# Attention scores from two float32r parts in two row groups, in place of three bf16 parts in one

## The chip, the cores and the metric

The kernel runs on one core of a Trainium2 chip. The metric is device time in microseconds of one launch, the median of several runs; lower is better. TensorE (PE) multiplies matrices, VectorE (DVE), ScalarE (ACT) and GpSimd (POOL) work on elements, and SyncE (SP) issues most DMAs.

## The reference

x has 4 batches of 1024 tokens of width 128. The layer is a macaron: half a mixture of experts, attention, half a mixture of experts again.

```python
x = x + 0.5 * ffn(layernorm(x), ...)      # 8 experts, top 1
q, k, v = (heads(layernorm(x) @ W.T) for W in (Wq, Wk, Wv))   # 16 heads of 8
q, k = rope(q), rope(k)
score = einsum('bqd,bkd->bqk', q, k), causal
out = softmax(score / sqrt(8)) @ v;   x = x + out @ Wo.T
x = x + 0.5 * ffn(layernorm(x), ...)
```

Everything is float32, and q and k have magnitudes at which a single bf16 product is too coarse for the scores. So the kernel splits q and k into parts whose products are exact, and adds the products in the contraction.

## The kernel before

**Three blocks run one after another**: the first expert layer (`ffn`, r=0), projection and attention (`project`, `attention`), and the second expert layer. The change touches the middle one alone, but for some memsets at the very start.

**Projection** (`project`) goes through 8 chunks of 512 tokens. PE turns a chunk (L947), multiplies it with four weight matrices for q and k (L957, float32) and one for v (L962). DVE multiplies with cosine and sine (`rotate`, L908 and L909), POOL adds the two (L1038), ACT copies the sum to bf16, which is the high part (L1008), DVE subtracts it from the sum (L917), ACT copies the rest to bf16, the middle part (L1014), and DVE (for q, L923) or POOL (for k, L1050) subtracts again for the low part. SP stores three parts of q and three of k to HBM in a layout by head (L1081).

**Attention** works in 16 stages of four heads (`QH`), each over all 1024 tokens. For a stage SP loads "stacks": `qs` and `ks` hold, for each head side by side in the free dimension, 72 rows (`PR`), in which the three parts of 8 rows are repeated so that each part of q meets each part of k. Three more rows (`MR`) of `qs` hold the negated row maximum in three bf16 parts, against ones in `ks`. Stacks have a ring of three.

Each stage does two things that are interleaved in one fixed order (`plan`):

- *tiles* for the next stage: PE computes scores with the queries on the partitions into one of two PSUM buffers `psS` (L1308), DVE adds the mask and takes the maximum of each row (L1448). There are 24 tiles: 8 of two heads with 128 to 512 keys each, 16 of one head with 640 to 1024 keys, the latter as two matmuls.
- *scores* for this stage: 12 units of 4 heads. PE computes scores transposed, maximum subtracted in the same contraction, into one of three buffers `psST` (L1339); ACT takes the exponential (L1412); POOL masks the diagonal (L1533); PE multiplies with v in float32, four heads in four groups of 32 columns (*weigh*, L1353), two units behind. ACT copies the sum out (L1418), PE turns it (L1323), DVE normalises (L1465, L1467).

POOL splits the row maxima (L1511 to L1516), PE turns them (L1316, *turn_max*), DVE copies them out (L1456), and SP moves them into the stacks' rows (`load_max`, L1272), twice a stage, once for each half of the queries. A score waits until the exponential three scores earlier is done (the buffers are three), a tile until the tile two earlier is read:

```python
                wait(pe, exp_done, s * SC + m - 2)
```
```python
        def use(index):
            wait(pe, use_read, index - 1)
```

The first score of each half waits for the maxima (`max_loaded`). Before the first stage an opening computes the tiles of stage 0; ahead of it stands a warm-up loop of fixed count on PE. ACT's first exponential waits until all parts are split (`lo_done`), because `prob` serves the projection as scratch.

Of the kernel before, what the change touches and what calls it, by code (L numbers as in the profile page):

```python
# [7 lines left out]
F32 = mybir.dt.float32  # L8
BF16 = mybir.dt.bfloat16
U32 = mybir.dt.uint32  # L10
# [22 lines left out]
KINDS = 3  # L33
PR = KINDS * KINDS * DK
MR = KINDS
CH = 512
# [121 lines left out]
def build(nc, x, Wp, Wr, br, ln, Wb1, W2, b2, const, tables, out):  # L158
    ctx = ExitStack()
    with ctx:  # L160
# [26 lines left out]

        n.ks = [sb(f"ks{i}", [PR + MR, QH * S], BF16) for i in range(RING)]
        n.qs = [sb("qs0", [PR + MR, QH * S], BF16)]
# [5 lines left out]

        n.q_dram = nc.dram_tensor("q_split", (KINDS * DK, NCH, B * H, CH), BF16, kind="Internal").ap()
        n.k_dram = nc.dram_tensor("k_split", (KINDS * DK, B * H, S), BF16, kind="Internal").ap()
# [41 lines left out]

def first_block_pool(nc, pool, n):  # L240
# [564 lines left out]
STACK_DMAS = 2 * KINDS - 1 + KINDS * NCH  # L805
# [3 lines left out]
def stack_parts(n, s, q, k):  # L809


    for c in range(KINDS):
        for first, last, at in ((c, KINDS, 0), (0, c, KINDS - c)):
            if first < last:
                here = c * PART_ROWS + at * DK
                yield (k[here:here + (last - first) * DK, :],
                       n.k_dram[first * DK:last * DK, ds(s * QH, QH), :].rearrange("d h t -> d (h t)"))
        for ch in range(NCH):
            yield (q[c * PART_ROWS:(c + 1) * PART_ROWS, ch * QH * CH:(ch + 1) * QH * CH],
                   n.q_dram[:, ch, ds(s * QH, QH), :].rearrange("d h t -> d (h t)"))  # L820
# [28 lines left out]
def project(nc, n, ctx, block):  # L849
# [7 lines left out]
    def sem(name):  # L857
# [7 lines left out]
    rot, tmp, rest = ([[n.prob[:, m, 2 * i + k, :] for k in range(2)] for i in range(2)] for m in range(3))  # L865
    part = [[sb(f"part{i}{k}", [P, KINDS, CH], BF16) for k in range(2)] for i in range(2)]
# [6 lines left out]
    proj_done, summed, hi_done, rest_done, mid_done = (  # L873
        [sem(f"{k}{i}") for i in range(2)] for k in ("proj_done", "summed", "hi_done", "rest_done", "mid_done"))
# [8 lines left out]
    def _(dve):  # L883
# [19 lines left out]
        def rotate(g, k):  # L903

            for i in range(2):
                dve.wait_ge(proj_done[i], g + 1)
                wait(dve, rest_done[i], g - 1)
# [71 lines left out]
    def _(act):  # L979
# [42 lines left out]
        for g in range(NC8):  # L1022
# [3 lines left out]
            if g >= 1:  # L1026
                mid(g - 1, (g - 1) % 2)
# [3 lines left out]
        mid(NC8 - 1, 1)  # L1031

    @block.gpsimd
    def _(pool):
# [5 lines left out]
        def subtract_hi(g, k):  # L1040
            for i in range(2):
                pool.wait_ge(hi_done[i], g + 1)
                pool.wait_ge(lo_done[i], g - 1)
                nc.gpsimd.tensor_tensor(rest[i][k], rot[i][k], part[i][k][:, 0, :],
                                        ALU.subtract).then_inc(rest_done[i], 1)

        def subtract_mid(g, k, i):

            pool.wait_ge(mid_done[i], g + 1)
            nc.gpsimd.tensor_tensor(part[i][k][:, 2, :], rest[i][k], part[i][k][:, 1, :],  # L1050
                                    ALU.subtract).then_inc(lo_done[i], 1)
# [3 lines left out]
        for g in range(NC8):  # L1055
            add_pairs(g, g % 2)
            if g >= 1:
                subtract_mid(g - 1, (g - 1) % 2, 1)
        subtract_mid(NC8 - 2, 0, 0)
        subtract_hi(NC8 - 1, 1)  # L1060
        for i in range(2):
            subtract_mid(NC8 - 1, 1, i)

    @block.sync
    def _(sp):
# [5 lines left out]
        def keep(g, k):  # L1071
            heads = slice((g - k) * (H // 2), (g - k) * (H // 2) + H)
            for i in range(2):
                sp.wait_ge(lo_done[i], g + 1)
                for m in range(KINDS):
                    rows = slice(m * DK, (m + 1) * DK)
                    if i == 0:
                        there = n.q_dram[rows, k, heads, :]
                    else:
                        there = n.k_dram[rows, heads, k * CH:(k + 1) * CH]  # L1080
                    sp.dma_start(there.rearrange("d h t -> h d t"), part[i][k][:, m, :]).then_inc(split_stored[i][k], 16)  # L1081
# [510 lines left out]
```

## Time and profile before

| | |
|---|---|
| median of 3 runs | 916.42 us (909.37 to 917.06) |
| profiled execution, first to last instruction | 855.6 us |
| outside of the span, median less span | 60.8 us |
| PE, DVE, ACT, POOL busy | 91%, 71%, 59%, 37% |
| mean granted TensorE clock | 0.945 |

The page gives one execution. The only time of that execution on record is its span; what lies around it is taken as the difference to the median. "L" numbers are lines of the kernel before. PEld is the loading of weights, which overlaps PE. A matmul's row lasts from its start to its modelled end, so that matmuls that follow each other overlap in the rows, and "x8" with one time is the union of eight. A busy PE is not necessarily a PE at its peak.

### The profile page before, as it was taken

What the parts mean: (1) busy time and instruction counts of PE and PEld (TensorE: products, weight loads), DVE (VectorE), ACT (ScalarE), POOL (GpSimd) and SP (SyncE); (2) the same over time, 40 slices, a digit from 0 to 9 for tenths busy, and PEclk for the clock granted to TensorE, in tenths of its full rate; (3) what the DMA queues carried; (4) which work ended last, traced back from release to release, by engine and by line L of the source; (5) the groups of instructions that cost most, each with busy time, mean ns of one, the idle gap of its engine ahead of it and who ended that gap; (6) DMA issues with size and microseconds to landing.
All of it is one profiled execution on the core that took longest, in us unless ns stands there. A gap on an engine that the chain in (4) does not pass through costs nothing. (4 is left out here: it accounts for less than half of the span.)

```text
span 855.6 us, 17846 instructions
## 1 busy us (share of the span) xinstructions
PE 779.7 (91%) x5570; PEld 427.9 (50%) x5570; DVE 610.9 (71%) x1919; ACT 507.4 (59%) x1229; POOL 315.4 (37%) x603
## 2 busy tenths in 40 slices
PE   9889999887899999999999999999999997689995
PEld 8888896543233333333333333333333335579884
DVE  4657774698668777788878878788787722856663
ACT  2166651673247767667667766766777684146662
POOL 6177742475104223223322422331242231056753
PEclk8699999998569999999999999999999998789998
DMA  8721113065332033033113303312320001122110
GB/s 271 270 57 50 54 33 117 23 169 159 57 57 45 14 57 57 10 49 58 34 26 57 53 6 57 58 22 36 57 41 18 3 1 34 73 70 50 52 42 26
DMA packets 27989, 51.84 MB, mean 61 GB/s; under 512 B 7552, under 2 KB 19200, under 8 KB 26496
## 3 DMA queue, kind: packets, MB, share of 16 engines
q1 hardware_dynamic: 21296, 41.04, 20.7%
q0 software_dynamic: 4096, 8.69, 3.8%
q10 hardware_dynamic: 2512, 1.06, 0.5%
q8 instruction: 43, 0.70, 0.4%
q14 instruction: 42, 0.34, 0.1%
HBM read 35.40 MB, written 14.97 MB: 59 GB/s over the span
## 5 line engine op out<-in xcount | busy, mean ns | idle before, releaser
L1448 DVE CUSTOM_DVE_ANT_0 cst<-psS,mask_row 128x768 bf16<-128x768 f32 (+7 forms) x512 | 364.7, 756 | 100.2 <-PE psS L1308 97.6
L1412 ACT ACTIVATE prob<-psST 128x512 f32<-128x512 f32 (+3 forms) x750 | 317.3, 495 | 158.9 <-PE psST L1339 155.2
L1353 PE MATMUL a_psO<-prob,vs 128*32 128x512 f32 (+3 forms) x1536 | 166.7, 506 | 2.8 <-ACT prob L1412 1.7
L1532 POOL TENSOR_TENSOR a_gate<-a_zeros 1x1 f32<-1x1 f32 x128 | 23.7, 185 | 333.7 <-ACT prob L1412 333.7
L1339 PE MATMUL psST<-a_qs,ks 75*128 75x512 bf16 (+1 forms) x480 | 123.7, 327 | 5.9 <-ACT prob L1412 3.5
L1308 PE MATMUL psS<-ks,a_qs 72*128 72x512 bf16 (+2 forms) x480 | 119.0, 337 | 5.6 <-DVE a_rowmax L1448 5.5
L777 POOL DMA_INDIRECT tok<-rows,f_there_number x64 | 61.8, 966 | 86.0 <-DVE f_number L489 42.0
L1308 PEld LDWEIGHTS psS<-ks,a_qs 72*128 72x128 bf16 x480 | 35.6, 99 | 101.1 <-DVE a_rowmax L1448 33.0
L1308 PE MATMUL psS<-ks,qs 72*128 72x512 bf16 (+3 forms) x288 | 75.8, 354 | 6.7 <-DVE a_rowmax L1448 6.5
L1533 POOL TENSOR_SCALAR_AFFINE_SELECT prob<-prob 128x512 f32<-128x512 f32 x128 | 80.3, 627 | 0.0
L1339 PE MATMUL psST<-qs,ks 75*128 75x512 bf16 (+3 forms) x270 | 73.4, 346 | 2.7 <-ACT prob L1412 1.7
L1339 PEld LDWEIGHTS psST<-a_qs,ks 75*128 75x128 bf16 x480 | 43.8, 97 | 61.4 <-ACT prob L1412 28.8
L726 ACT ACTIVATE f_xnT<-f_ps_half,gb 128x128 f32<-128x128 f32 x64 | 29.3, 458 | 54.4 <-PE f_ps_half L654 54.4
L522 DVE TENSOR_SCALAR f_hidT<-f_ps_wide,f_w1s 128x128 f32<-128x128 f32 x156 | 47.2, 345 | 18.0 <-PE f_ps_logit L663 13.7
L663 PE MATMUL f_ps_wide<-f_xnT,f_w1s 128*128 x312 | 49.7, 282 | 10.0 <-ACT f_hidT L734 5.4
L743 ACT ACTIVATE f_w1s<-w 128x516 f32 x78 | 49.7, 637 | 9.8 <-DVE f_item_ring L479 9.3
L1353 PEld LDWEIGHTS a_psO<-prob,vs 128*32 128x32 f32 x1536 | 30.6, 108 | 48.1 <-ACT prob L1412 31.6
L1308 PEld LDWEIGHTS psS<-ks,qs 72*128 72x128 bf16 x288 | 21.6, 100 | 64.5 <-DVE a_rowmax L1448 28.4
L663 PEld LDWEIGHTS f_ps_wide<-f_xnT,f_w1s 128*128 128x128 f32 x312 | 40.9, 191 | 14.1 <-issue 14.0
L673 PE MATMUL f_ps_rank<-w,f_hidT 128*128 x320 | 45.4, 285 | 0.3 <-DVE f_hidT L522 0.3
L1339 PEld LDWEIGHTS psST<-qs,ks 75*128 75x128 bf16 x270 | 25.6, 102 | 38.8 <-ACT prob L1412 17.9
L1448 DVE DVE_READ_ACCUMULATOR2_ANT a_rowmax<- 128x1 f32 x512 | 42.6, 83 | 0.0
(183 smaller groups left out, 1066.1 us busy)
## 6 DMA issues: line engine op xcount, KB each, us to landing
a_qs<-q_split SPq DMA_DIRECT2D x60, 96.0 KB
rows<-tok SPq DMA_DIRECT2D x8, 536.0 KB, 4.9
ks<-k_split SPq DMA_DIRECT2D x32, 128.0 KB
qs<-q_split SPq DMA_DIRECT2D x36, 96.0 KB
q_split<-p_part SPq DMA_DIRECT2D x24, 128.0 KB, 2.4
k_split<-p_part SPq DMA_DIRECT2D x24, 128.0 KB, 2.4
ks<-k_split SPq DMA_DIRECT2D x16, 192.0 KB
tok<-x_after_first SPq DMA_DIRECT2D x4, 536.0 KB, 5.4
```

The costliest lines, as they stand in the source:

```text
L522: last = nc.vector.tensor_scalar(hidT[i % 2][:, f * P:(f + 1) * P], hidden_at(i, f), w1s[i % 4][:, F + f:F + f + 1], 0.0, ALU.add, ALU.max)
L663: last = nc.tensor.matmul(hidden_at(i, f), w1s[i % 4][:, f * P:(f + 1) * P], xnT[:, ds(slot_of[i], 1), :], start=True, stop=True)
L673: last = nc.tensor.matmul(psY[i % 2], hidT[i % 2][:, f * P:(f + 1) * P], n.w2[:, ds(expert[i], 1), f * D:(f + 1) * D], start=(f == 0), sto ...
L726: nc.scalar.activation(xnT[:, t % XR, :], psX[t % 2], ACT.Identity, bias=n.gb[:, 1:2], scale=n.gb[:, 0:1]).then_inc(x_ready, 1)
L743: nc.scalar.activation(w1s[i % 4][:, :], n.w1[:, ds(expert[i], 1), :], ACT.Copy).then_inc(w1_ready, 1)
L777: pool.indirect_dma_start(out=row[:, t, :], out_offset=None, in_=n.rows_dram[r][:, :], in_offset=bass.IndirectOffsetOnAxis(ap=there_number ...
L1308: last = nc.tensor.matmul(ps[:, a * CH + c0:a * CH + c0 + w], lhs, ks[r][0:PR, h * S + c0:h * S + c0 + w], start=True, stop=True)
L1339: nc.tensor.matmul(score_buffer(s, m)[:, 0:w], ks[r][:, h * S + j * P:h * S + (j + 1) * P], qs[r][:, q_col(h, q0):q_col(h, q0) + w], start ...
L1353: last = nc.tensor.matmul(psO[32 * h:32 * h + 32, c0:c0 + w], vs[r][:, j, h, :], prob[:, u % RING, h, 0:w], start=(j == 0), stop=(u + 1 in ...
L1412: nc.scalar.activation(prob[:, u % RING, h, 0:w], score_buffer(s, u * QH + h)[:, 0:w], ACT.Exp, scale=SCALE).then_inc(exp_done, 1)
L1448: last = nc.vector.tensor_tensor_reduce(out=out[:, a * CH:a * CH + width], in0=ps[:, a * CH:a * CH + width], in1=mask_row[:, S - width:], ...
L1533: nc.gpsimd.affine_select(out=part, in_=part, compare_op=ALU.is_ge, fill=0.0, base=0, pattern=[[0, QH], [1, P]], channel_multiplier=-1).th ...
```

## The change

q and k are split into two parts of the type float32r (the high part rounded to 12 bits, and the rest), so four products of 8 rows, 32 rows, stand for one head. `KINDS` is 2. A 33rd row holds zero in `qs` (and one in `ks`), and two rows (33 and 34) take the maximum in two float32r parts. Each stack tensor now has 128 partitions: heads 0 and 2 of a stage lie in rows 0 to 34, heads 1 and 3 in rows 64 to 98, two heads behind one another in the free dimension. So matmuls of neighbouring heads use different row groups of 64 rows. All matmuls have the same columns as before, and PE's order of work is the same.

In the projection the middle part goes (L1014, L923, L1050), and one subtraction each is left for q (DVE) and for k (POOL). Parts are stored as 4-byte values.

```diff
-KINDS = 3
-PR = KINDS * KINDS * DK
+KINDS = 2
+PR = KINDS * KINDS * DK + 1
 MR = KINDS
+SIDES = 2
+SIDE = P // SIDES
+SH = QH // SIDES
...
-        n.ks = [sb(f"ks{i}", [PR + MR, QH * S], BF16) for i in range(RING)]
+        n.ks = [sb(f"ks{i}", [P, SH * S], F32R) for i in range(RING)]
...
     link = Chain(pool, n.ring_init)
+    for a in range(SIDES):
+        link(nc.gpsimd.memset(n.qs[0][zero_row(a), :].bitcast(F32), 0.0))
     for r in range(RING):
-        link(nc.gpsimd.memset(n.ks[r][64:PR + MR, :], 1.0))
+        for a in range(SIDES):
+            link(nc.gpsimd.memset(n.ks[r][a * SIDE + PR - 1:a * SIDE + PR + MR, :].bitcast(F32), 1.0))
...
-STACK_DMAS = 2 * KINDS - 1 + KINDS * NCH
+STACK_DMAS = SIDES * (2 * KINDS + 1)
...
         def subtract_hi(g, k):
-            for i in range(2):
-                dve.wait_ge(hi_done[i], g + 1)
-                wait(dve, lo_done[i], g - 1)
-                nc.vector.tensor_tensor(rest[i][k], rot[i][k], part[i][k][:, 0, :],
-                                        ALU.subtract).then_inc(rest_done[i], 1)
-
-        def subtract_mid(g, k):
-
-            dve.wait_ge(mid_done[0], g + 1)
-            nc.vector.tensor_tensor(part[0][k][:, 2, :], rest[0][k], part[0][k][:, 1, :],
+            dve.wait_ge(hi_done[0], g + 1)
+            nc.vector.tensor_tensor(part[0][k][:, 1, :], rot[0][k], part[0][k][:, 0, :].bitcast(F32),
                                     ALU.subtract).then_inc(lo_done[0], 1)
...
-        def mid(g, k):
-
-            for i in range(2):
-                act.wait_ge(rest_done[i], g + 1)
-                nc.scalar.activation(part[i][k][:, 1, :], rest[i][k], ACT.Copy).then_inc(mid_done[i], 1)
-
...
         def load_max(s, r, half):
 
             sp.wait_ge(maxT_ready, 2 * s + half + 1)
-            sp.dma_start(max_rows(r, half), maxT[half][:, :]).then_inc(max_loaded[half], 16)
+            for k in range(QH):
+                a, g = k // SH, k % SH
+                sp.dma_start(max_rows(r, half, g * SIDES + a),
+                             maxT[half][k * MR * CB:(k + 1) * MR * CB, :].bitcast(F32)).then_inc(max_loaded[half], 16)
...
-                lhs = qs[r][0:PR, q_col(h, i * P):q_col(h, i * P) + P]
+                lhs = qs[r][side(h, PR), q_col(h, i * P):q_col(h, i * P) + P]
...
-                                            ks[r][0:PR, h * S + c0:h * S + c0 + w], start=True, stop=True)
+                                            ks[r][side(h, PR), q_col(h, c0):q_col(h, c0) + w], start=True, stop=True)
...
-            nc.tensor.transpose(ps[:, 0:P // 2].bitcast(BF16), maxparts[:, :], n.identb[:, :]).then_inc(use_done, 1)
+            nc.tensor.transpose(ps[:, 0:P], maxparts[:, :].bitcast(F32), n.c("ident")).then_inc(use_done, 1)
...
-            nc.tensor.matmul(score_buffer(s, m)[:, 0:w], ks[r][:, h * S + j * P:h * S + (j + 1) * P],
-                             qs[r][:, q_col(h, q0):q_col(h, q0) + w], start=True, stop=True).then_inc(scored, 1)
+            nc.tensor.matmul(score_buffer(s, m)[:, 0:w], ks[r][side(h, PR + MR), q_col(h, j * P):q_col(h, j * P) + P],
+                             qs[r][side(h, PR + MR), q_col(h, q0):q_col(h, q0) + w],
+                             start=True, stop=True).then_inc(scored, 1)
...
         pool.wait_ge(cleared, 1)
+        pool.wait_ge(n.lo_done[1], NC8)
+        clear = Chain(pool, rows_cleared)
+        for r in range(1, RING):
+            for a in range(SIDES):
+                clear(nc.gpsimd.memset(qs[r][zero_row(a), :].bitcast(F32), 0.0))
```

On SP's queue the two loads of maxima between the stacks of two stages stand before as the first, and in the changed kernel as the second of these (`a_maxT` to the stacks, then the stacks of a later stage):

```order
L1272 DMA a_qs<-a_maxT 3x16x128 x2
L826 DMA ks<-k_split 24x4096
L826 DMA a_qs<-q_split 24x2048 x2
L826 DMA ks<-k_split 16x4096
L826 DMA ks<-k_split 8x4096
```
```order
L1266 DMA a_qs<-a_maxT 2x4x128 x8
L842 DMA ks<-k_split 16x2x1024
L842 DMA ks<-k_split 8x2x1024 x2
L842 DMA qs<-q_split 16x2x1024 x2
L842 DMA ks<-k_split 16x2x1024
```

Each load of maxima has become four issues, which stand ahead of the same stack loads; a stack has ten issues in place of eleven.

On POOL the end of the projection and the beginning of attention read as follows, before and after:

```order
L1050 TENSOR_TENSOR p_part<-prob,p_part 128x512 x2
L1044 TENSOR_TENSOR prob<-prob,p_part 128x512 x2
L1050 TENSOR_TENSOR p_part<-prob,p_part 128x512 x2
L1492 UNCONDITIONAL_BRANCH
L1550 COPY vs<-vals 128x32x8
L1511 TENSOR_TENSOR a_maxparts<-a_zeros,a_rowmax 128x16
```
```order
L1042 TENSOR_TENSOR p_part<-prob,p_part 128x512
L1042 TENSOR_TENSOR shared<-prob,shared 128x512
L1487 UNCONDITIONAL_BRANCH
L1545 MEMSET a_qs 1x2048 x4
L1547 COPY vs<-vals 128x32x8
L1507 TENSOR_TENSOR a_maxparts<-a_zeros,a_rowmax 128x4x4
```

Four subtractions at the end have gone, and four memsets of one row stand in front of the first copy of v.

## Rows read from the trace of the kernel before

**Rows 1.** The page: the span, and PE's granted clock in 40 slices

```profile
span 855.6 us, 17846 instructions
...
PEclk8699999998569999999999999999999998789998
```

**Rows 2.** Busy time by stretch: us, PE, PEld, DVE, ACT, POOL, then clock, DMA share, GB/s

```profile
215.00:262.00 47.00, 43.62 (x184) 13.80 (x184) 32.73 (x86) 19.39 (x42) 6.97 (x23) 0.63 0.30 52
...
300.00:660.00 360.00, 343.30 (x2402) 126.21 (x2395) 286.87 (x822) 250.95 (x593) 102.13 (x318) 1.00 0.24 41
```

**Rows 3.** Waits from 300 to 660 us: total, times, longest

```profile
ACT prob L1412 <- PE psST L1339: 100.1, 145, 1.3
...
PEld psS L1308 <- DVE a_rowmax L1448: 34.4, 47, 0.8
PEld psST L1339 <- ACT prob L1412: 33.8, 94, 0.6
```

**Rows 4.** PE in order of time, in the middle stages: start, length, what

```profile
272.53 0.34 PE L1339 MATMUL psST<-a_qs,ks 75*128 75x128 bf16 x3
...
274.38 0.81 PE L1339 MATMUL psST<-a_qs,ks 75*128 75x512 bf16 x3
...
275.58 0.66 PE L1323 MATMUL psS<-cst,p_anT 128*128 128x128 f32 x4
276.07 0.38 PE L1339 MATMUL psST<-a_qs,ks 75*128 75x512 bf16 x1
...
329.70 0.22 PE L1316 MATMUL psS<-identb,a_maxparts 128*128 128x128 bf16 x1
...
330.12 1.07 PE L1353 MATMUL a_psO<-prob,vs 128*32 128x512 f32 x8
331.12 0.50 PE L1308 MATMUL psS<-ks,a_qs 72*128 72x384 bf16 x2
...
450.94 0.22 PE L1316 MATMUL psS<-identb,a_maxparts 128*128 128x128 bf16 x1
```

**Rows 5.** The page's groups of attention: busy, mean ns, idle before

```profile
L1448 DVE CUSTOM_DVE_ANT_0 cst<-psS,mask_row 128x768 bf16<-128x768 f32 (+7 forms) x512 | 364.7, 756 | 100.2 <-PE psS L1308 97.6
L1412 ACT ACTIVATE prob<-psST 128x512 f32<-128x512 f32 (+3 forms) x750 | 317.3, 495 | 158.9 <-PE psST L1339 155.2
```

**Rows 6.** PE in order of time in the first router: moving 8 columns, float32 weights

```profile
11.23 0.96 PE L592 MATMUL f_ps_logit<-wrc,f_xT 128*128 128x8 f32 x8
```

**Rows 7.** PE and DVE in order of time, in the projection

```profile
169.96 1.09 PE L962 MATMUL psST<-wall,p_anT 128*128 128x136 f32 x8
172.00 0.66 PE L947 MATMUL psST<-cst,p_an 128*128 128x128 f32 x4 [0.95 <-ACT p_an L985]
172.49 3.60 PE L957 MATMUL psS<-p_anT,wall 128*128 128x512 f32 x8
...
175.62 0.68 DVE L908 TENSOR_TENSOR prob<-psS,cst 128x512 f32<-128x512 f32 x1
...
181.58 0.68 DVE L908 TENSOR_TENSOR prob<-psS,cst 128x512 f32<-128x512 f32 x1
```

**Rows 8.** POOL in order of time: the first memset, the first split of maxima

```profile
0.80 3.50 POOL L244 MEMSET ks<- 11x4096 bf16 x1 [0.29 <-POOLq L1585]
...
209.91 0.22 POOL L1511 TENSOR_TENSOR a_maxparts<-a_zeros,a_rowmax 128x16 bf16<-128x16 f32 x1 [1.20 <-DVE a_rowmax L1448]
```

**Rows 9.** In order of time from 300 us: SP's DMA issues, PE's first score

```profile
300.42 0.70 SPq L1272 DMA_DIRECT2D a_qs<-a_maxT  x1
...
301.17 0.45 SPq L826 DMA_DIRECT2D ks<-k_split  x1
301.67 0.76 SPq L826 DMA_DIRECT2D a_qs<-q_split  x2
...
303.53 0.38 PE L1339 MATMUL psST<-a_qs,ks 75*128 75x512 bf16 x1
```

**Rows 10.** The page's DMA issues: KB each, us to landing

```profile
k_split<-p_part SPq DMA_DIRECT2D x24, 128.0 KB, 2.4
```

More of the change, by code:

```diff
@@ L9 @@
 BF16 = mybir.dt.bfloat16
+F32R = mybir.dt.float32r
 U32 = mybir.dt.uint32
@@ L802, in ffn, with heads, rows @@
         return rows_written
-STACK_DMAS = 2 * KINDS - 1 + KINDS * NCH
+STACK_DMAS = SIDES * (2 * KINDS + 1)
 PART_ROWS = KINDS * DK
 def stack_parts(n, s, q, k):
[L812 to L820, printed above, removed]
+    def heads(source, first, last, a):
+        return source[first * DK:last * DK, ds(s * QH, QH), :].rearrange("d (g a) t -> a d g t", a=SIDES)[a]
+    def rows(stack, a, at, count):
+        here = a * SIDE + at * DK
+        return stack[here:here + count * DK, :].bitcast(F32).rearrange("d (g t) -> d g t", g=SH)
+    for a in range(SIDES):
+        yield rows(k, a, 0, KINDS), heads(n.k_dram, 0, KINDS, a)
+        for c in range(KINDS):
+            yield rows(k, a, KINDS + c, 1), heads(n.k_dram, KINDS - 1 - c, KINDS - c, a)
+        for c in range(KINDS):
+            yield rows(q, a, c * KINDS, KINDS), heads(n.q_dram, 0, KINDS, a)
 def load_stacks(sp, n, s, q, k, loaded):
@@ L863, in project @@
     n.outT = anT[0]
-    rot, tmp, rest = ([[n.prob[:, m, 2 * i + k, :] for k in range(2)] for i in range(2)] for m in range(3))
-    part = [[sb(f"part{i}{k}", [P, KINDS, CH], BF16) for k in range(2)] for i in range(2)]
+    rot, tmp = ([[n.prob[:, m, 2 * i + k, :] for k in range(2)] for i in range(2)] for m in range(2))
+    free = n.shared[:, NT // 2:, :].rearrange("p (i a) d -> p i (a d)", i=2).bitcast(F32R)
+    part = [[sb(f"part{i}", [P, KINDS, CH], F32R), free[:, i, :].rearrange("p (m t) -> p m t", m=KINDS)] for i in range(2)]
     psA, psV = n.psST[0], n.psST[1:3]
@@ L1030, in _ @@
             hi(g, g % 2)
-        mid(NC8 - 1, 1)
     @block.gpsimd
@@ L1040, in subtract_hi @@
         def subtract_hi(g, k):
[L1041 to L1051, printed above, removed]
+            pool.wait_ge(hi_done[1], g + 1)
+            nc.gpsimd.tensor_tensor(part[1][k][:, 1, :], rot[1][k], part[1][k][:, 0, :].bitcast(F32),
+                                    ALU.subtract).then_inc(lo_done[1], 1)
         nc.gpsimd.memset(n.mask_row[:, 0:S - P], 0.0).then_inc(n.mask_made, 1)
@@ L1057, in _ @@
             if g >= 1:
[L1058 to L1062, printed above, removed]
+                subtract_hi(g - 1, (g - 1) % 2)
+        subtract_hi(NC8 - 1, (NC8 - 1) % 2)
     @block.sync
@@ L1076, in keep @@
                     rows = slice(m * DK, (m + 1) * DK)
[L1077 to L1081, printed above, removed]
+                    there = (n.q_dram, n.k_dram)[i][rows, heads, k * CH:(k + 1) * CH]
+                    sp.dma_start(there.rearrange("d h t -> h d t"), part[i][k][:, m, :].bitcast(F32)).then_inc(split_stored[i][k], 16)
         for g in range(EARLY):
@@ L1206, in q_col, with side @@
     def q_col(h, q):
-        return (q // CH * QH + h) * CH + q % CH
+        return h // SIDES * S + q
+    def side(h, rows):
+        return slice(h % SIDES * SIDE, h % SIDES * SIDE + rows)
     def sb(name, shape, dt=F32):
@@ L1217, in sem @@
         return ctx.enter_context(nc.semaphore(f"a_{name}"))
-    qs = n.qs + [sb(f"qs{i}", [PR + MR, QH * S], BF16) for i in range(1, RING)]
+    qs = n.qs + [sb(f"qs{i}", [P, SH * S], F32R) for i in range(1, RING)]
     ks, vs = n.ks, n.vs
@@ L1330, in score @@
                 half = half_start.index(u)
-                pe.wait_ge(max_loaded[half], (s + 1) * 16)
+                pe.wait_ge(max_loaded[half], (s + 1) * 16 * QH)
             m = u * QH + h
@@ L1454, in copy_max @@
             dve.wait_ge(use_done, index + 1)
-            wait(dve, max_loaded[half], s * 16)
-            nc.vector.tensor_copy(maxT[half][:, :],
-                                  ps[0:MP, 0:P // 2].bitcast(BF16)).then_inc(use_read, 1)
+            wait(dve, max_loaded[half], s * 16 * QH)
+            nc.vector.tensor_copy(maxT[half][:, :], ps[0:MP, 0:P]).then_inc(use_read, 1)
             dve.wait_ge(use_read, index + 1)
@@ L1502, in split @@
             wait(pool, maxT_ready, 2 * s + half)
-            src = rowmax[:, :, half * CB:(half + 1) * CB]
-            done = order * 4
+            src = rowmax[:, :, :, half * CB:(half + 1) * CB]
+            done = order * 2
             def link(ins, k):
```

62 lines of the change are left out of this document (30 added, 32 removed).

## The prediction

> **What bounds the kernel now.** I read the slices first: PE is granted full speed from the projection on, but for the slices in which attention opens [rows 1]. By stretch, PE is busy 343 of 360 us in the middle of attention, DVE 287, ACT 251 [rows 2]. The period comes from two turns of maxima four stages apart, 329.70 and 450.94 [rows 4]: **30.31 us per stage**. So DVE works 24.2 and ACT 21.1 us per stage, nearly all of it the reading of tiles (364.7 / 16 = 22.8) and the exponentials (317.3 / 16 = 19.8) [rows 5].
>
> PE's own work per stage, from the distances between starts [rows 4]. A score of 512 columns takes (0.81 - 0.38) / 2 = 0.215 us and one of 128 about 0.06, which is one column per 2.4 GHz cycle and some 0.005 us each. A *weigh* takes 331.12 - 330.12 = 1.00 us for 512 columns; its four passes are 4 x 512 / 2400 = 0.853, so 0.147 goes in changing to the column groups and back. The 12 units have 4608 columns:
> - weigh: 4 x 4608 / 2400 + 12 x 0.147 = 9.4;
> - 48 scores with 18432 columns: 7.7 + 0.2 = 7.9; 48 tile matmuls with as many: 7.9;
> - two turns of the output at 0.49 and two turns of maxima: 1.3.
>
> Together 26.5, so PE stands 3.8 us per stage. The waits say on whom: on DVE's reading of a tile buffer and on the exponential three scores back, while ACT waits on PE for 100 us of the 360 [rows 3]. PE is the longest, but the period is made by three engines that wait for one another in one fixed order.
>
> **The change, part by part.**
>
> *Scores and tiles.* What a float32r column costs, no row shows. The near end is that of bf16, one cycle. The far end is two, as of every 4-byte operand that streams here: the turn of the output takes 0.11 us for 128 columns, 0.49 for four with the change of kind [rows 4]. I take one cycle, because a float32 matmul of 512 columns, which does four products per value, takes 2 x 0.43 = 0.86 us = 4 cycles per column [rows 7], so one product is one cycle; the turn moves values in full width. The Trainium skill (FP8 and Floating Point Precision, TensorE Precision Notes) has full float32 as four passes and a reduced kind that reads four bytes and truncates; by it a single pass is one cycle as well, and the sum stays.
>
> That two row groups run side by side I take from the column groups: four heads' float32 matmuls, eight records, are done in 1.07 us [rows 4], the time of one. Between two weighs or turns I added the columns by side: 36864 columns in all, 21760 on the longer sides, so at most 6.3 us are saved. But PE starts matmuls in order, and a one-head tile has both its matmuls on one side; stepping through the order with that rule leaves 4.5. The turns of maxima and output now change the kind too, four a stage at about 0.2: +0.8. PE's own work falls to **22.8**.
>
> The Trainium skill (TensorE: Matmul & The Clock Gate, Part 3) gives 3.07 for four row tiles in place of one; halving scores and tiles by such a rule would take 7.9 off instead of 4.5. It also says (Weight-path perf modes) that fast weight load is not for FP32, which speaks against the change. The row that bears on it: eight loads of float32 weights with 8 columns behind each take 0.96, 0.10 to 0.11 us a load [rows 6], where bf16 loads fit into 0.06 [rows 4]. I carry 0.06 to 0.11 for a load that must wait for another.
>
> *What of this reaches the period.* Not 3.7 us. I stepped through one stage in the order of the program: each instruction starts when its engine is free and what it waits for is done, with the distances above, ACT at 0.49 us per 512 columns, DVE at 1.15 per 1024, and POOL. For the kernel before this gives 29.95 (30.31 measured), with 2.4 us of PE's waits. With sides it gives **29.7, 30.0 or 30.5** for loads of weights at 0, 0.06 and 0.11. PE's waits grow from 2.4 to 6.0: the second turn of maxima 0.4 to 0.9 and tile 18 0.4 to 0.7 (both for DVE), scores 1.2 to 3.4 in all (for ACT). Whenever PE gets ahead, it stands at the third score buffer or the second tile buffer, behind it in the queue stand the weigh and the tile that the other engine needs, and the order gives the time back. I take 30.0 against 29.95: +0.05 x 14 middle stages = **+1**; ends -4 and +8.
>
> *Opening and first stage.* The clock is at 1.2 GHz in much of 215 to 262 us (0.63 on average) [rows 2], and there PE is the limit. Stepping with doubled PE times gives 51.8 before and 45.2 to 47.2 after per stage; about two thirds of such a stage: **-4**.
>
> *Projection.* DVE sets the period of a chunk, 181.58 - 175.62 = 5.96 us [rows 7]. It loses two of four subtractions. Next is PE: 3.43 + 0.93 + 0.49 and some switching = 5.0 [rows 7]. Over the last 5 or 6 chunks 0.9 each: **-5**. POOL and ACT lose more than they need. Stores grow from 768 to 1024 KB per chunk, in four issues instead of six. They hide behind 5 us as they hid behind 6; without that cover +2.
>
> *POOL's memsets.* 11 rows x 4096 bf16 took 3.50 [rows 8], so 2048 values about 1.8, or 2 if float32 is slower. Eight at the start, 15 us, are over long before the first gather. Four, about 8 us, follow POOL's last subtraction and precede the first split, which before had 1.2 us of idle ahead of it [rows 8]. What pays is that POOL now ends two subtractions and a copy sooner after the last rotation, 6 us; with the idle that covers it: 0, and +1 without.
>
> *The maxima's loads.* One issue of 0.70 becomes four; later issues follow in 0.4 to 0.5 [rows 9], so the last is about 1.0 later. The first half's load began at 300.42 and the score that needs it at 303.53, 3.1 us later; a DMA of this queue lands in 2.4 [rows 9, 10]. Slack about 0.7: 0, and 14 x 0.3 = +4 if it is short. POOL's split is two operations shorter.
>
> **Sum.** +1 - 4 - 5 = -8. The profiled execution's span is 855.6 [rows 1], so 848 after; the median of the runs is 60.8 above the span, and I keep that distance: 916.4 - 8 = **908 us**. A measurement of this kernel tells about 1% (9 us) from no change.
>
> **Rivals.**
> 1. *The forecast*, 898 to 918: chance 0.42, half of it beyond 1%.
> 2. *Each float32r matmul costs more than its columns* (weights at 0.11 that nothing hides, short matmuls that take as long as one of 512): stepping gives +1.1 us per stage, 15 - 8: 923. For it: the 0.11 [rows 6]. Against: loads of different groups start together in the weigh. 0.22.
> 3. *It gets slower: two cycles per column.* PE's stream for scores and tiles doubles to 31 us, of which pairs hide part; stepping gives 36.9 to 37.6 per stage. 14 x 7 = 98, 4 more in the last stage, less the projection's 5: 1013. It decides from about 1.1 cycles per column on. For it: the turns at two [rows 4]. Against: the four passes in four cycles. 0.14.
> 4. *The waits don't come back.* If PE waited as long as now, a stage would take 22.8 + 3.8 = 26.6, never under DVE's 24.2; a fourth of that gain, 0.9 to 1.0 us x 14, gives 895, all of it 856. For it: my stepping may bind engines tighter than the chip. 0.17.
> 5. *The clock.* With a third of PE's time idle it could stay at 1.2 GHz past the opening, each such stage +16 us. Above 940. 0.05. Against: 31 of the 40 slices are granted 90% or more, whatever the block [rows 1].
>
> **Numbers.** Likeliest 908. Range **888 to 942**: the first two, most of the fourth and the doubts on cover; left out are the third, the fifth and the best of the fourth, some 0.2. Faster by over 1%: 0.21 + 0.17 = 0.38. Within: 0.21 + 0.14 = 0.35. Slower: 0.08 + 0.14 + 0.05 = 0.27.
>
> **What would show it.** Score matmuls of two sides start some ns apart when both buffers are free, and 512 columns take 0.215 per side (0.43 says the third case). DVE and ACT as before per instruction; the period between turns of maxima near 30.3. PE's waits on ACT and DVE about doubled. The projection's period 5.0 to 5.3. The first score of a half waits for exponentials, not for a DMA. If PE's share stays at 95% with the same period, my columns are wrong; if the period falls under 29, my stepping is.

## The result, and the profile after

| | before | changed |
|---|---|---|
| median of the runs | 916.35 us (909.37 to 917.06) | 1183.28 us (1179.14 to 1187.18) |
| ratio | | 1.294, 95% interval 1.287 to 1.301 |
| profiled execution, span | 855.6 us | 1185.5 us |
| mean granted TensorE clock | 0.945 | 0.636 |

The prediction was 908 us, 888 to 942. The kernel became 29% slower. The first thing to read is the page's span and the row of the granted clock, against [rows 1]:

```profile
span 1185.5 us, 17812 instructions
...
PEclk7788999855555555555555555555585555877899
```

From the ninth slice on, where attention opens, the clock is 5 tenths, which is 1.2 GHz, through the whole of attention but for one slice. Before, two slices of attention were low. The same by stretch (columns as in [rows 2]): projection, opening, middle of attention, and the one full stretch:

```profile
178.00:218.00 40.00, 37.78 (x159) 22.46 (x157) 23.75 (x38) 25.48 (x74) 28.39 (x21) 1.00 0.58 158
240.00:262.00 22.00, 19.89 (x88) 10.76 (x87) 16.95 (x54) 5.86 (x16) 3.83 (x12) 0.50 0.49 65
300.00:660.00 360.00, 345.79 (x1461) 151.26 (x1461) 176.49 (x511) 156.87 (x364) 56.92 (x169) 0.50 0.17 24
870.00:890.00 20.00, 16.43 (x120) 7.65 (x116) 15.58 (x42) 12.99 (x31) 4.45 (x13) 1.00 0.01 2
```

PE is as busy as before, 346 of 360 us, but with 1461 matmuls in place of 2402 [rows 2]. DVE and ACT lost over a third of their busy time per us. Their instructions did not become slower, they came more rarely, as the page's groups show against [rows 5]:

```profile
L1444 DVE CUSTOM_DVE_ANT_0 cst<-psS,mask_row 128x768 bf16<-128x768 f32 (+7 forms) x512 | 364.9, 755 | 354.2 <-PE psS L1303 353.8
L1408 ACT ACTIVATE prob<-psST 128x512 f32<-128x512 f32 (+3 forms) x750 | 324.3, 492 | 409.3 <-PE psST L1334 405.9
```

Busy time and mean are those of before within 3%, the idle time ahead of them has more than tripled for DVE, and PE ends it. So PE bounds attention now. The period, from PE in order of time (two turns of maxima with one more between them, which is one stage; and neighbouring rows at either clock):

```profile
451.01 0.47 PE L1311 MATMUL psS<-cst,a_maxparts 128*128 128x128 f32 x1
...
489.07 0.79 PE L1303 MATMUL psS<-ks,a_qs 33*128 33x512 f32 x1
489.08 0.58 PE L1334 MATMUL psST<-a_qs,ks 35*128 35x256 f32 x1
...
500.98 0.47 PE L1311 MATMUL psS<-cst,a_maxparts 128*128 128x128 f32 x1
...
872.16 0.49 PE L1303 MATMUL psS<-ks,a_qs 33*128 33x512 f32 x1
872.17 0.50 PE L1334 MATMUL psST<-qs,ks 35*128 35x512 f32 x1
```

**49.97 us per stage** in place of 30.31. The two sides do run beside one another: a tile and a score of different sides start 0.01 us apart, at 489 as at 872. So the sides work as planned, and the clock fell. Fourteen stages at 19.66 more are 275 us.

### The profile page after: what moved, and what is told of

Read it like the earlier page. It is cut to its first block and busy times, and to the rows that moved or that the text cites. A ratio compares the mean times of both kernels' runs of the same rounds, so it can differ in the third digit from the quotient of the medians.

```text
span 1185.5 us, 17812 instructions
## 1 busy us (share of the span) xinstructions
PE 1067.0 (90%) x5570; PEld 603.8 (51%) x5570; DVE 600.3 (51%) x1907; ACT 505.5 (43%) x1213; POOL 307.1 (26%) x544
## 5 line engine op out<-in xcount | busy, mean ns | idle before, releaser
L1349 PE MATMUL a_psO<-prob,vs 128*32 128x512 f32 (+3 forms) x1536 | 280.5, 822 | 1.6 <-POOL prob L1525 1.0
L1334 PE MATMUL psST<-a_qs,ks 35*128 35x512 f32 (+1 forms) x480 | 229.7, 603 | 8.1 <-ACT prob L1408 8.1
L1303 PE MATMUL psS<-ks,a_qs 33*128 33x512 f32 (+3 forms) x480 | 163.1, 579 | 8.4 <-DVE a_rowmax L1444 8.4
L1303 PEld LDWEIGHTS psS<-ks,a_qs 33*128 33x128 f32 x480 | 89.4, 303 | 148.8 <-issue 90.2
L1334 PEld LDWEIGHTS psST<-a_qs,ks 35*128 35x128 f32 x480 | 124.7, 307 | 71.5 <-ACT prob L1408 50.6
L1334 PE MATMUL psST<-qs,ks 35*128 35x512 f32 (+3 forms) x270 | 122.7, 584 | 4.5 <-ACT prob L1408 4.3
L1303 PE MATMUL psS<-ks,qs 33*128 33x512 f32 (+3 forms) x288 | 101.2, 588 | 8.0 <-DVE a_rowmax L1444 7.9
L1303 PEld LDWEIGHTS psS<-ks,qs 33*128 33x128 f32 x288 | 54.8, 307 | 88.6 <-issue 49.7
L1334 PEld LDWEIGHTS psST<-qs,ks 35*128 35x128 f32 x270 | 65.6, 291 | 43.0 <-ACT prob L1408 29.4
L675 PEld LDWEIGHTS f_ps_wide<-f_xnT,f_w1s 128*128 128x128 f32 x312 | 46.0, 212 | 41.9 <-issue 41.6
L685 PE MATMUL f_ps_number<-w,f_hidT 128*128 x304 | 45.5, 298 | 0.0
```

Of the source, the lines that this page charges most:

```text
L675: last = nc.tensor.matmul(hidden_at(i, f), w1s[i % 4][:, f * P:(f + 1) * P], xnT[:, ds(slot_of[i], 1), :], start=True, stop=True)
L685: last = nc.tensor.matmul(psY[i % 2], hidT[i % 2][:, f * P:(f + 1) * P], n.w2[:, ds(expert[i], 1), f * D:(f + 1) * D], start=(f == 0), sto ...
L1303: last = nc.tensor.matmul(ps[:, a * CH + c0:a * CH + c0 + w], lhs, ks[r][side(h, PR), q_col(h, c0):q_col(h, c0) + w], start=True, stop=True)
L1334: nc.tensor.matmul(score_buffer(s, m)[:, 0:w], ks[r][side(h, PR + MR), q_col(h, j * P):q_col(h, j * P) + P], qs[r][side(h, PR + MR), q_col ...
L1349: last = nc.tensor.matmul(psO[32 * h:32 * h + 32, c0:c0 + w], vs[r][:, j, h, :], prob[:, u % RING, h, 0:w], start=(j == 0), stop=(u + 1 in ...
```

## The experiments

Times of single runs stand beside a run of the kernel before on the same chip, at 906 to 913 us; effects under 1% are not read from them. A granted clock between 0.50 and 1.00 is a mean: part of the stretch at 1.2 GHz, part at 2.4.

**e5: the kernel before once more**, unchanged.

> The kernel before, unchanged, for a trace beside a time of the same execution: the profiled execution of before had a span of 855.6 us, its runs lie at 909 to 917, and the profiled execution of the changed kernel has a span of 1185.5 for a run of 1187.18. Theory 'around the span' (the prediction's: some 60 us lie outside the span): a span near 855 for a time near 910. Theory 'another execution' (the first profile was a quicker one than the runs timed): a span 2 us under the time, near 905 to 915, the attention as before with 30.31 us per stage at a clock of 1.0, and the 50 us more in the two expert blocks, at a lower granted clock.

Measured: 910.14 us with a span of 908.4. What lies around the span is 2 us, not 60. This execution's rows (the sources of the exponential and of the rotation, with their first and last start; then the stretch):

```profile
L1412 ACT ACTIVATE prob<-psST x750: 271/575/642, 246.6 to 738.4; 128x512 f32<-128x512 f32 x94, 128x128 f32<-128x128 f32 x32, 128x384 f32<-128x384 f32 x31, 128x256 f32<-128x256 f32 x31
...
L908 DVE TENSOR_TENSOR prob<-psS,cst x16: 673/679/692, 177.9 to 222.7; 128x512 f32<-128x512 f32 x16
```

```profile
300.00:660.00 360.00, 342.90 (x2395) 126.18 (x2394) 287.25 (x830) 251.88 (x593) 101.90 (x321) 1.00 0.24 41
```

and the same two sources in the changed kernel:

```profile
L1408 ACT ACTIVATE prob<-psST x750: 272/584/658, 242.0 to 1014.1; 128x512 f32<-128x512 f32 x94, 128x128 f32<-128x128 f32 x32, 128x384 f32<-128x384 f32 x31, 128x256 f32<-128x256 f32 x31
...
L925 DVE TENSOR_TENSOR prob<-psS,cst x16: 690/691/692, 179.4 to 217.2; 128x512 f32<-128x512 f32 x16
```

So e5 is the execution to subtract. The spans differ by 1185.5 - 908.4 = 277.1 us: attention from the first exponential to the last 772.1 against 491.8, **+280.3**; projection from the first to the last chunk 37.8 against 44.8, **-7.0**; the rest +3.8. The 53 us by which the first profile was quicker lie in the two expert blocks (its first rotation stands at 150.81, here at 177.9), and attention took 491.9 there as well.

**Which theory of the clock?** The change did three things to PE's work in attention: fewer *rows* under each matmul (33 and 35 for 72 and 75), two of them side by side, so that PE has more time without any (*waits*), and another *type*. Four kernels separate them.

e1: more rows, and nothing else.

```diff
-PR = KINDS * KINDS * DK + 1
+PR = 62
...
-    return slice(a * SIDE + PR - 1, a * SIDE + PR)
+    return slice(a * SIDE + KINDS * KINDS * DK, a * SIDE + PR)
...
-            link(nc.gpsimd.memset(n.ks[r][a * SIDE + PR - 1:a * SIDE + PR + MR, :].bitcast(F32), 1.0))
+            link(nc.gpsimd.memset(n.ks[r][a * SIDE + KINDS * KINDS * DK:(a + 1) * SIDE, :].bitcast(F32), 1.0))
```

> The changed kernel with more rows under every score and tile, and nothing else: the maxima move to rows 62 and 63 of a side, rows 32 to 61 are zero in qs and one in ks, so a tile contracts over 62 rows and a score over 64 per side, in place of 33 and 35. Same columns, same order, same results. Theory 'rows' (TensorE is granted 2.4 GHz according to how much of the array works, and 33 to 35 rows per matmul are too few): the granted clock is 1.0 from the end of the opening on, the period of a stage falls from 49.97 to 30 to 32.5 us, time 900 to 955. Theory 'waits' (it is PE's time without any matmul that keeps the clock low, since two sides finish together): clock 0.5, period 50, time 1183. Theory 'type' (float32r itself keeps it low): 0.5 and 1183 too.

e2: one side alone. Heads 1 and 3 take the scores of heads 0 and 2, and their own are left out.

```diff
     def side(h, rows):
-        return slice(h % SIDES * SIDE, h % SIDES * SIDE + rows)
+        return slice(0, rows)
```

> The changed kernel with all four heads read from side 0: heads 1 and 3 take the scores of heads 0 and 2 (their own are left out). Same type, same rows (33 and 35), same columns, but no two matmuls of scores or tiles side by side. Theory 'waits': PE streams without pause as in the kernel before, the clock is 1.0 past the opening, the period 30 to 31 us, time 905 to 935. Theory 'rows': 33 to 35 rows at a time are even less than two times 33 to 35; the clock stays at 0.5, and the period is PE's own work at that clock, 2 x 26.5 = 53 us in place of 49.97, time 1220 to 1250. Theory 'type': the same 0.5 and 1220 to 1250.

e3: bf16 for float32r (the bitcasts to F32 go, and the maxima are turned as in the kernel before; a third part of q, k and the maxima is left out).

```diff
-F32R = mybir.dt.float32r
+F32R = mybir.dt.bfloat16
```

> The changed kernel with bf16 for float32r everywhere (stacks, parts, maxima), two sides of 33 and 35 rows as in the change; the scores are those of two bf16 parts, the third part is left out. Theory 'type': clock 1.0 past the opening, period 29.5 to 30.5, time 900 to 920. Theories 'rows' and 'waits': clock 0.5, period 49 to 50, time 1165 to 1185.

e4: the kernel before with fewer rows (q, k and the maxima are still split in three, and the third part is left out).

```diff
-KINDS = 3
+KINDS = 2
...
-        link(nc.gpsimd.memset(n.ks[r][64:PR + MR, :], 1.0))
+        link(nc.gpsimd.memset(n.ks[r][PR:PR + MR, :], 1.0))
...
-            sp.dma_start(max_rows(r, half), maxT[half][:, :]).then_inc(max_loaded[half], 16)
+            sp.dma_start(max_rows(r, half), maxT[half][0:MR * QH * CB, :]).then_inc(max_loaded[half], 16)
```

> The kernel before with two bf16 parts in the stacks in place of three, one row group: 32 rows under a tile and 34 under a score in place of 72 and 75, everything else as before (the third part of q, k and the maxima is computed but left out of the scores). Theory 'rows': clock 0.5 from the opening on, period 2 x 26.5 = 53 us, time 1220 to 1260. Theories 'waits' and 'type': nothing that the clock depends on has changed, clock 1.0, period 30.3, time 905 to 920.

Measured: e1 963.16, e2 1319.1, e3 1085.03, e4 1215.98 us. The row of 300 to 660 us of each, in this order; the granted clock is the third number from the end:

```profile
300.00:660.00 360.00, 309.77 (x2136) 145.35 (x2135) 257.44 (x734) 226.42 (x526) 79.80 (x237) 0.96 0.24 33
```
```profile
300.00:660.00 360.00, 359.79 (x1280) 194.03 (x1278) 158.27 (x451) 142.33 (x318) 50.34 (x151) 0.50 0.13 19
```
```profile
300.00:660.00 360.00, 336.29 (x1698) 84.50 (x1693) 203.41 (x583) 179.82 (x420) 63.95 (x191) 0.55 0.05 14
```
```profile
300.00:660.00 360.00, 357.54 (x1401) 75.06 (x1400) 172.89 (x485) 153.36 (x348) 59.80 (x187) 0.56 0.06 11
```

*Waits* falls: in e2 PE is busy for all of the 360 us at 0.50, in e1 it stands 50 of them at 0.96. *Type* falls as the cause: e4 has no float32r and one row group, and attention slows from 491.8 to 794.3 us. *Rows* stands: adding rows under the same matmuls brings the clock back (e1), taking rows from the kernel before takes it away (e4). In e4 another cost comes on top: a change between matmuls of 32 and of 34 rows costs some 0.13 us at 1.2 GHz (0.56 from a tile of 512 columns to the next score, where the 512 columns themselves take 0.43).

The clocks fell out as *rows* has them, but no time lies in its range. e1 is 8 us over it, since its clock is not quite 1.00 and float32r has a price of its own (below). e2 is 69 over it, at 57 us per stage where doubling gave 53; e3 is 80 under it, since at the same clock bf16 needs less time per stage, and part of its attention is at 2.4 GHz. e4 is 4 under it. The type is thus not what brings the clock down, but it is a cost beside it. It may shift the clock a little as well: 0.55 in e3 for 0.50 in the changed kernel.

**How far does it hold?** e8 is e1 on one side (heads 1 and 3 again take the scores of heads 0 and 2), e9 is e4 with the rows of e1 (62 and 64).

```diff
     def side(h, rows):
-        return slice(h % SIDES * SIDE, h % SIDES * SIDE + rows)
+        return slice(0, rows)
```

> Kernel e1 with all heads read from side 0, as in e2 (heads 1 and 3 take the scores of heads 0 and 2): one group of 62 and 64 rows at a time, PE streaming without pairs. Against e2 only the rows differ, 62 and 64 for 33 and 35. Theory 'rows': the clock is mostly 1.0, as with the 72 and 75 rows of before; the period is that of one side at full clock, 30.3 plus what float32r costs, 32 to 34, time 940 to 980. If two sides at once are needed for it (128 rows in all): clock 0.5, period 57.2 as in e2, time 1300 to 1320.

```diff
-PR = KINDS * KINDS * DK
+PR = 62
...
-        link(nc.gpsimd.memset(n.ks[r][PR:PR + MR, :], 1.0))
+        link(nc.gpsimd.memset(n.ks[r][32:PR + MR, :], 1.0))
+        if r == 0:
+            link(nc.gpsimd.memset(n.qs[0][32:PR + MR, :], 0.0))
...
+        for r in range(1, RING):
+            clear(nc.gpsimd.memset(qs[r][32:PR + MR, :], 0.0))
```

> The kernel before with two bf16 parts in the stacks (as e4: the third part is computed and left out) and 62 and 64 rows under a tile and a score, one row group: rows 32 to 61 are zero in qs and one in ks. Against e8 only the type differs (bf16 for float32r), against e4 only the rows (62 and 64 for 32 and 34). Theory 'rows alone': as in e8, three quarters of attention at 1.2 GHz, time 1080 to 1130. Theory 'rows and pace' (what counts is how much of the array works per us, and float32r's longer weight loads thin it out: e8 needs 57.2 us per stage at 1.2 GHz where the kernel before needs some 52): clock 1.0 as with the 72 and 75 rows of before, period 30.3, time 905 to 925.

Measured: e8 1183.17, e9 1001.75 us. Both lie between their theories. e8's clock is 0.62 from 300 to 660 us against e2's 0.50 with half the rows. e9 does the same work for 14 stages, and is granted two clocks:

```profile
300.00:480.00 180.00, 179.02 (x708) 53.64 (x707) 85.61 (x251) 76.69 (x176) 32.24 (x102) 0.50 0.07 13
490.00:660.00 170.00, 161.92 (x1120) 57.66 (x1121) 133.46 (x390) 118.00 (x278) 48.69 (x152) 1.00 0.10 17
```

It stays at 1.2 GHz from the opening on for 256 us, rises, and stays up to the end of attention, at 52.65 and 30.75 us per stage. So the same work can keep either level, and the time of such a kernel hangs on how long it keeps the lower one. The number of rows alone does not settle the level; why e9 rose when it did, no run shows. Between e8 and e9 the type differs, but not only it: float32r also spreads the matmuls (33.9 against 30.75 us per stage at full clock). The two effects were not taken apart.

**e11: more work in place of more rows.**

```diff
+            if h == 0:
+                for _ in range(4):
+                    nc.tensor.matmul(score_buffer(s, m)[:, 0:P], n.onesb[:, :], n.onesb[:, :], start=True, stop=True)
             nc.tensor.matmul(score_buffer(s, m)[:, 0:w], ks[r][side(h, PR + MR), ...
```

> The changed kernel with work that nobody needs: ahead of the first score of every unit four bf16 matmuls of 128 rows and 128 columns into the same buffer, which the score then overwrites. Results unchanged, 768 more matmuls, at full clock 12 x (4 x 0.055 + two changes of kind at about 0.13) = 5.8 us more of PE's time per stage. Theory 'how much of the array works': the clock rises for at least part of attention, and the kernel with more work is quicker than the changed one: 1000 to 1150. If only the rows of the scores and tiles themselves decide: clock 0.5, the fillers come on top at half clock, 16 x 8 to 11 us: 1310 to 1360.

Measured: 1306.35 us, a clock of 0.50 from 300 to 660 and 56.93 us per stage. My favoured theory missed: 12 x 512 more columns a stage with all rows, beside 36864 with few, did not lift it, and cost 7.0 us per stage. That is one dose of one kind of work. It does not tell whether the clock goes by the rows of the tiles and scores themselves or by a sum over all matmuls that this dose left too small.

**e12: zeros on both sides of the added rows.** In e1 the added rows multiply a zero by a one.

```diff
+            link(nc.gpsimd.memset(n.ks[r][zero_row(a), :].bitcast(F32), 0.0))
```

> Kernel e1 with zeros in both operands of the added rows: rows 32 to 61 of a side are zero in qs and now in ks too (ones there in e1). Theory 'rows count, whatever is in them': as e1, clock 0.90, time 955 to 970. Theory 'values' (rows count by what moves through them, and e1's ones did it): the clock goes back towards 0.64, time above 1050.

Measured: 989.18 us at 0.868, 26 above e1. To see what that is worth, and to price the type at one clock, three kernels were timed in rounds: e13 is e1, e15 is e12, and e14 is e1 in bf16, which had been run once as e7.

> Kernel e1 (two sides, 62 and 64 rows) with bf16 for float32r; the third part of q, k and the maxima is left out. It prices the type at the same clock. If the clock follows the rows: 1.0 or a short dip per stage, as in e1. If the type costs nothing at the full clock: period 34.1 as in e1 and the same 963. If the longer weight load of float32r (records of 0.183 against 0.098 us) and the change from a score to a weigh (0.42 against 0.31 us from start to start) cost it: period 29.3 to 30.5, time 895 to 915.

> Kernel e1 again, timed in rounds beside e14 and e15 on one chip. e1 gave 963.16 in one run. If the clock's pattern in attention (a dip of 3.4 us once per stage) belongs to the kernel: 960 to 966. If it differs by execution: a spread of 15 us or more.

> Kernel e7 (e13 in bf16 with two parts) again, in rounds. The difference to e13 prices float32r with the rows, the order and the sides equal. If it is the weight loads and the changes from scores to weighs alone (about 1.9 us per stage) and the dips of the clock (1.7 per stage): e13 less e14 = 14 x 3.4 = 45 to 50 us, e14 at 912 to 920, ratio to before 0.998 to 1.005.

> Kernel e12 (e13 with zeros in both operands of the added rows) again, in rounds. If values count a little: it stays 20 to 30 us above e13 in every run. If the 26 us between e12 and e1 were a difference between executions: within 10 us of e13.

Measured: e7 916.36; e13 974.24 (966.34 to 979.51), ratio 1.065, interval 1.058 to 1.071; e14 913.78 (907.86 to 917.37), ratio 1.001, interval 0.998 to 1.004; e15 984.36 (961.06 to 993.48). e12 came out between its two theories. e13 and e15 overlap: e15's quickest is under all of e13, its other three are above all of e13. So rows of zeros count for the clock nearly as much as any, and whether values matter a little stays open. e13's runs lie 13 us apart and above the 966 that a fixed pattern would have given, so its clock differs somewhat by execution. e13 and e14 differ by 60 us, where I expected 45 to 50. Turns of maxima one stage apart at full clock, first e13, then e14:

```profile
419.41 0.33 PE L1311 MATMUL psS<-cst,a_maxparts 128*128 128x128 f32 x1 [0.76 <-DVE a_rowmax L1444]
...
430.64 0.47 PE L1334 MATMUL psST<-a_qs,ks 64*128 64x512 f32 x1 [0.35 <-ACT prob L1408]
431.04 0.64 PE L1349 MATMUL a_psO<-prob,vs 128*32 128x256 f32 x8
...
452.50 0.33 PE L1311 MATMUL psS<-cst,a_maxparts 128*128 128x128 f32 x1 [0.78 <-DVE a_rowmax L1444]
```
```profile
425.72 0.39 PE L1334 MATMUL psST<-a_qs,ks 64*128 64x512 bf16 x1
426.04 1.06 PE L1349 MATMUL a_psO<-prob,vs 128*32 128x512 f32 x8
...
456.65 0.23 PE L1311 MATMUL psS<-identb,a_maxparts 128*128 128x128 bf16 x1 [0.68 <-DVE a_rowmax L1444]
...
487.19 0.23 PE L1311 MATMUL psS<-identb,a_maxparts 128*128 128x128 bf16 x1 [0.68 <-DVE a_rowmax L1444]
...
518.35 0.23 PE L1311 MATMUL psS<-identb,a_maxparts 128*128 128x128 bf16 x1 [0.68 <-DVE a_rowmax L1444]
```

33.09 us in e13; in e14 stages of 30.54 and of 31.16 us take turns. So float32r costs **2 to 2.6 us per stage** at full clock. A score of 512 columns is followed by the weigh after 0.40 us, in bf16 after 0.32; twelve of these are 1.0 of it. The loads of weights (e13, e14; mean length is the last number before the idle time):

```profile
L1334 PEld LDWEIGHTS psST<-a_qs,ks 64*128 64x128 f32 x70 | 11.2, 184 | 8.8 <-ACT prob L1408 6.5 <-issue 0.6 <-DMA a_qs<-a_maxT 0.6
```
```profile
L1334 PEld LDWEIGHTS psST<-a_qs,ks 64*128 64x128 bf16 x46 | 3.7, 93 | 7.5 <-ACT prob L1408 5.3 <-issue 0.9
```

0.184 against 0.093 us, and in e8 two scores of 128 columns on one side start 0.11 us apart where the kernel before has 0.055. Fourteen stages make 27 to 36 of the 60 us. The rest is the clock: from the first to the last exponential e13 is granted 0.89 and e14 0.96, which is some 120 and 40 us at 1.2 GHz. With 50 us for a stage at 1.2 GHz and 33 at full clock, 80 us more there lose about 27, an estimate from these rows.

**e6 and e10: the kernel before with more rows.** If rows hold the clock, the opening of the kernel before should gain.

```diff
-PR = KINDS * KINDS * DK
+PR = 125
...
         link(nc.gpsimd.memset(n.ks[r][64:PR + MR, :], 1.0))
+        if r == 0:
+            link(nc.gpsimd.memset(n.qs[0][64:PR + MR, :], 0.0))
...
+        sp.wait_ge(rows_cleared, RING - 1)
         load(1, 1)
...
+        for r in range(1, RING):
+            clear(nc.gpsimd.memset(qs[r][64:PR + MR, :], 0.0))
         pool.wait_ge(n.v_copied, NC8)
```

> The kernel before (three bf16 parts, one row group) with all 128 rows under every matmul of attention: rows 72 to 124 are zero in qs and one in ks, the maxima move to rows 125 to 127, so a tile contracts over 125 rows and a score over 128. Two more memsets stand on POOL ahead of the loads of the second stack. Theory 'rows': the stretch at 1.2 GHz in the opening becomes shorter, the period stays 30.3, time 5 to 15 us under the kernel before. Theory 'data' (what counts is work on values other than zero): the opening as before, time within 3 us of before.

Measured: 910.69 us, within 3 of before, as theory *data* had it, but only because two terms cancel. Attention itself took 483.5 us for 491.8, and the opening lost 4.4 of it: on PE, in order of time, the first turn of maxima waits for POOL, which is at its two memsets (7.07 us).

```profile
239.42 1.46 PE L1311 MATMUL psS<-ks,qs 125*128 125x512 bf16 x4 [0.30 <-DVE a_rowmax L1451]
246.63 0.27 PE L1319 MATMUL psS<-identb,a_maxparts 128*128 128x128 bf16 x1 [5.75 <-POOL a_maxparts L1519]
```

In e10 these two memsets stand behind the first split:

```diff
         split(0, 0, HALF_TILES, 0)
+        pool.wait_ge(split_done, 1)
...
+        for r in range(1, RING):
+            clear(nc.gpsimd.memset(qs[r][64:PR + MR, :], 0.0))
```

> Kernel e6 (the kernel before with 125 and 128 rows under its matmuls) with the two added memsets moved on POOL from ahead of the first split of maxima to behind it. In e6 attention itself was 8.3 us shorter than in e5, and the memsets put the first turn of maxima off (PE idle 5.75 us before it). If both hold: 7 to 10 us under before, ratio 0.989 to 0.993. If the shorter stretch at 1.2 GHz in e6 came from the later start and not from the rows: ratio 0.998 to 1.002.

Measured: **905.1 us** (902.65 to 909.68), ratio 0.992, interval 0.988 to 0.996. The opening, in e5 and in e10:

```profile
240.00:262.00 22.00, 18.97 (x66) 5.98 (x68) 15.46 (x40) 6.13 (x16) 3.56 (x13) 0.50 0.33 58
```
```profile
240.00:262.00 22.00, 17.97 (x82) 5.46 (x80) 18.13 (x51) 5.86 (x16) 11.42 (x17) 0.73 0.44 86
```

More rows, the same columns, and the clock is 0.73 for 0.50; from 222 to 277 us it is 0.84 for 0.57, and attention takes 484.3 us for 491.8. This beats both kernels, by rows that compute nothing. The gain is 0.8%, small, but clear of the noise: seven runs against twelve of the kernel before on one chip.

## Why the prediction was wrong

**The step that failed is the fifth rival, its condition and its chance.** I asked of the clock only how much of the time PE is busy, took "31 of the 40 slices are granted 90% or more, whatever the block" as evidence against, and gave 0.05. In the changed kernel PE is busy 96% of the middle at half clock, in e14 81% at 0.98. What I should have asked is what each matmul uses of the array: the change cut the rows by half under most of attention's columns. The blocks that ran at full clock on [rows 1] had 72 to 128 rows under every matmul, so the row spoke of no case like this one. The same evidence could have been read as a warning, since the opening of the same kernel, with the same 72 rows, already fell to 0.63 [rows 2]. The Trainium skill (TensorE: Matmul & The Clock Gate, Part 1) ties the gate to how busy PE has been; busy time alone does not explain e2, where PE is busy 360 of 360 us at 0.50. I also gave the rival the wrong condition, a third of PE's time idle: PE was idle for 4%.

**The rival's price was too low.** I had 16 us for each such stage, from doubled PE times; it is 19.66. The same kernel in bf16 (e3) needs 44.95 at 1.2 GHz, near the 45.2 of my stepping; float32r takes the other 5.0.

**Scores and tiles: right but for the type.** One column per cycle holds: in e2 matmuls of 512 columns on one side start 0.427 us apart, which is 512 cycles of 1.2 GHz. So the third rival falls. Two sides run side by side. But a load of float32r weights is twice that of bf16, and a stage at full clock takes 33.1 (e13) where I had 30.5 for loads at 0.11 and 31.1 in the second rival. The step "I carry 0.06 to 0.11 for a load that must wait" had the right load and missed the longer way from score to weigh and, on one side, 0.229 to 0.237 for 0.215 to 0.220 per 512 columns (e8). Even with its rows filled up and the clock at 0.94, the change is 6.5% slower (e13). The Trainium skill (TensorE: Matmul & The Clock Gate, Weight-path perf modes) says that fast weight load is not for FP32; 0.184 against 0.093 agrees with that.

**"Not 3.7 us", the waits give it back: right in the main.** e14 has the sides without float32r, at 0.98 of full clock. PE works 291 of 360 us for 343, and the period is 30.54 to 31.16 for 30.31. Its waits, against [rows 3]:

```profile
ACT prob L1408 <- PE psST L1334: 106.7, 164, 2.0
...
PEld psST L1334 <- ACT prob L1408: 59.8, 92, 0.9
PEld psS L1303 <- DVE a_rowmax L1444: 57.6, 77, 1.2
...
PEld psST L1334 <- DMA a_qs<-a_maxT: 9.8, 7, 1.9
...
PE psST L1334 <- DMA a_qs<-a_maxT: 7.4, 7, 1.6
PE psST L1334 <- DMA qs<-a_maxT: 2.8, 3, 1.4
```

The waits of PE's weight loads for ACT and DVE nearly doubled, ACT's on PE did not shrink. The last two lines are a wait that the kernel before does not have: the scores stand for the maxima, 10.2 us of the 360, or 0.9 per stage. Even if all of it came back, a stage would take some 30.0 us, an estimate, and not 26.6; so the fourth rival falls in its full form. Whether its small form, a gain of a fourth, would show with a shorter load of the maxima was not run. As the kernel stands, pairs gain nothing.

**Projection: -7.0 for -5.** DVE's rotations of the changed kernel, against [rows 7]:

```profile
191.89 0.69 DVE L925 TENSOR_TENSOR prob<-psS,cst 128x512 f32<-128x512 f32 x1 [1.20 <-PE psS L965]
...
196.69 0.69 DVE L925 TENSOR_TENSOR prob<-psS,cst 128x512 f32<-128x512 f32 x1 [1.20 <-PE psS L965]
```

The period is 4.80 where I added PE up to 5.0.

**The maxima's loads: mis-sized.** I had the last of four about 1.0 us later. On SP's queue the four take 2.57 us, where one took 0.70, so the last is 1.9 later:

```profile
501.85 2.57 SPq L1266 DMA_DIRECT2D a_qs<-a_maxT  x4
```

At half clock nobody waits for them; in e14 PE does, 0.9 us per stage (above), where I had 0, or 0.3 if the slack was short. The price there was not run alone.

**POOL's memsets: 7.37 us, and near nothing.** The split follows at once, and the way from the last rotation to the first exponential is 24.8 us for 24.0 in e5.

```profile
224.87 7.37 POOL L1545 MEMSET a_qs<- 1x2048 f32 x4
...
232.66 0.21 POOL L1507 TENSOR_TENSOR a_maxparts<-a_zeros,a_rowmax 128x16 fp32r<-128x16 f32 x1
```

**Opening and first stage: -4, and nothing came.** The first turn of maxima and the third lie 42.4 us apart in the changed kernel and 41.9 in e5: the first half was 1.6 shorter, and the second lost it again. The two were not at one clock there: in the second half e5 was granted 0.62, the changed kernel 0.50. So this term too fell to the clock.

**Outside of the span: wrong, without effect on the sum.** The 60.8 us were a quicker profiled execution, not time around it (e5).

## What to carry to other kernels

Before cutting the contraction of a matmul, count the rows of the array that stay in use as well as the columns and the busy time, and read the granted clock of the stretch: here 33 to 35 rows in place of 72 to 75 cost 280 us of attention, and zero rows up to 64 on each side brought back 212 of them (e13, first to last exponential 560.5 us) at no time per matmul (matmuls of 512 columns start 0.427 us apart with 33 to 35 rows in e2 and with 62 to 64 in e8, both at 1.2 GHz). When a slowdown is spread evenly over all of PE's instructions while those of other engines keep their length, look at the clock first. A split into float32r parts saves rows and element work, not PE time: its weights load at half the pace of bf16 (0.184 us for 0.093).

## What the runs showed of the hardware

- Granted clock from 300 to 660 us, by rows under tiles and scores: 33 and 35 on one side, float32r, 0.50; on two sides 0.50, and in bf16 0.55; 32 and 34 in bf16 0.56; 62 and 64 on one side 0.62 in float32r, 0.74 in bf16; on two sides 0.94 to 0.96 in float32r (0.87 to 0.90 with both operands zero), 0.97 to 0.98 in bf16; 72 and 75, and 125 and 128, 1.00.
- The same instructions can run for hundreds of us at either level (e9), or rise for 20 us and fall back (the changed kernel at 870 to 890 us).
- Rows whose operands are both zero count nearly as the others do (e12, e15).
- Loads of maxima in four issues in place of one kept PE waiting 0.9 us per stage at 0.98 of full clock (e14), and not at 1.2 GHz (the changed kernel).
- Changing between matmuls of 32 and of 34 rows cost some 0.13 us at 1.2 GHz (e4).
